# Column sums of the odd units on GpSimd, and seven split units instead of three, in the first product of a graph network

## The reference

```
h = relu(layernorm(x)); x = x + relu([h, adj @ h] @ W.T + b)           # layer 0
h = relu(layernorm(x)); a = adj + I; d = rsqrt(sum(a, axis=-1))        # layer 1
x = x + unit_rows((a * d[:, None] * d[None, :]) @ h @ W.T + b)
h = relu(layernorm(x)); x = x + GRU(relu(adj @ h @ Wm.T + bm), h)      # layer 2
h = relu(layernorm(x)); z, its 4 nearest rows of all 4096,             # layer 3
x = x + d2 * ((S + adj) @ (d2 * h)) @ W2 + b2
```

## Time and profile before

| | before |
|---|---|
| median of three runs | 1536.28 us |
| profiled execution, from its first to its last instruction (its span; no other time of it is given) | 1534.6 us |
| first product, block period of blocks 1 to 7 | 29.95 us |
| busy over the span: TensorE, VectorE, ScalarE, GpSimd | 96%, 78%, 52%, 12% |
| in a block of the first product: TensorE, VectorE, ScalarE | 29.95, 26.84, 6.17 us |

### The profile page before, as it was taken

How to read it: one execution, slowest core, us unless ns; L and a number is a source line. 1 busy time by engine, 2 the same in 40 slices (tenths; PEclk the granted TensorE clock), 3 DMA queues, 4 the chain that set the end, 5 groups by cost and what they waited for, 6 DMA issues and landing times.

```text
span 1534.6 us, 18912 instructions
## 1 busy us (share of the span) xinstructions
PE 1466.8 (96%) x4982; PEld 841.8 (55%) x4982; DVE 1193.8 (78%) x1644; ACT 797.9 (52%) x1243; POOL 191.1 (12%) x205
## 2 busy tenths in 40 slices
PE   7999999999999999999999999999999999698894
PEld 4555555677776667666766662222222224466662
DVE  7899989878787776677778776888888887576784
ACT  3212223566666666566565644445455545566673
POOL 0000000000000000000000000000000000888886
PEclk9999999999999999999999999999999999899997
DMA  8788888898898677777898990000000006889992
GB/s 306 253 284 273 286 277 290 311 328 329 330 339 333 239 282 281 271 255 272 302 336 324 336 334 24 0 7 7 7 7 7 7 0 223 286 312 331 337 344 95
DMA packets 99515, 351.64 MB, mean 229 GB/s; under 512 B 12704, under 2 KB 12832, under 8 KB 99488
## 3 DMA queue, kind: packets, MB, share of 16 engines
q1 hardware_dynamic: 94752, 340.83, 62.3%
q0 software_dynamic: 4736, 10.49, 2.0%
HBM read 347.08 MB, written 4.19 MB: 229 GB/s over the span
## 4 chain that ended last, share of the span: by engine, by line
PE 81%; POOL 11%; issue 5%; DMA 1%; DVE 1%; ACT 0%; POOLq 0%; SPq 0%; ACTq 0%
PE ps L529 17%; PE ps L354 12%; PE ps L386 11%; POOL landing L1151 10%; PE ps L390 9%; PE ps L392 9%; PE ps L391 8%; PE ps L530 5%; PE ps L448 1%; PE ps L414 1%; PE ps L474 1%; PE ps L475 1%; POOL picks L1148 1%; PE ps L421 1%; PE ps L347 1%
## 5 line engine op out<-in xcount | busy, mean ns | idle before, releaser
L981 DVE TENSOR_TENSOR A_lo<-ring,A_hi 128x1024 fp32r<-128x1024 f32 x411 | 488.6, 1220 | 137.7 <-ACT A_hi L573 125.5
L573 ACT ACTIVATE A_hi<-ring 128x1024 fp32r<-128x1024 f32 x411 | 425.0, 1055 | 151.3 <-PE ps L392 83.9
L390 PE MATMUL ps<-A_hi,G_odd_hi 128*128 128x512 f32 x588 | 268.3, 456 | 36.6 <-DVE A_lo L981 35.7
L392 PE MATMUL ps<-A_hi,G_odd_lo 128*128 128x512 f32 x588 | 235.5, 401 | 0.0
L391 PE MATMUL ps<-A_lo,G_odd_hi 128*128 128x512 f32 x588 | 235.1, 400 | 0.0
L354 PE MATMUL ps<-ring,G_first 128*128 128x512 f32 x428 | 190.7, 592 | 0.0
L1055 DVE MAX8 rows_T<-scores 128x8 f32<-128x4096 f32 x32 | 141.7, 4428 | 57.9 <-ACT scores L573 57.9
L386 PE MATMUL ps<-ring,G_whole 128*128 128x512 f32 x384 | 180.4, 592 | 0.0
L1140 POOL DMA_DIRECT2D scaled_rows<-G_last x8 | 6.2, 780 | 1291.1 <-ACT G_last L573 1291.1
L1151 POOL DMA_INDIRECT landing<-scaled_rows,picks x128 | 159.4, 1246 | 35.0 <-issue 30.7
L390 PEld LDWEIGHTS ps<-A_hi,G_odd_hi 128*128 128x128 f32 x588 | 114.1, 194 | 87.8 <-issue 38.5
(11 more groups left out here) (143 smaller groups left out, 1547.5 us busy)
## 6 DMA issues: line engine op xcount, KB each, us to landing
ring<-adj_t SPq DMA_DIRECT2D x640, 512.0 KB
X<-x_rows SPq DMA_DIRECT2D x8, 256.0 KB, 7.9
scaled_rows<-G_last POOLq DMA_DIRECT2D x8, 256.0 KB, 2.7
landing<-scaled_rows,picks POOLq DMA_INDIRECT x128
out_rows<-X SPq DMA_DIRECT2D x8, 256.0 KB
pack<-packed SPq DMA_DIRECT2D x1, 836.0 KB, 13.7
pack<-packed SPq DMA_DIRECT2D x1, 192.0 KB, 3.3
```

Source lines behind the costliest of these rows:

```text
L390: mm(acc, G_hi[odd][:, m, kk, :], hi, start=begin, stop=False)
L392: last = mm(acc, G_lo[odd][:, m, kk, :], hi, start=False, stop=end)
L573: return nc.scalar.activation(out_ap, in_ap, func, **k)
L981: v.tensor_tensor(A_lo[:, slot, :, :], ring[:, u % SLOTS, :, :], A_hi[:, slot, :, :].bitcast(fp32), ALU.subtract).then_inc(lower_ready, 1)
```

## The change

The odd units leave VectorE's loop. GpSimd gets a loop of its own, `sum_odd_pieces`, whose first instruction adds units 1 and 3 into the second half of `colsum`, and six further ones add units 5 to 15 (one instruction of 128 x 1024 for each). The one semaphore `summed` becomes `even_summed` (raised by VectorE in steps of 2) and `odd_summed` (raised by GpSimd, by 4 for the first, by 2 for each later one). The loads of odd slots wait for `odd_summed`. The first product splits seven units of blocks 1 to 7 instead of three, all of them odd. Two tables of steps change with it.

```diff
-SPLIT_FIRST = (7, 10, 14)
+SPLIT_FIRST = (1, 3, 5, 7, 9, 11, 13)
...
-                    sp.wait_ge(summed, last + 1)
+                    sp.wait_ge(odd_summed if u % 2 else even_summed, last + 1)
...
                 for u in range(UNITS):
-                    dve.wait_ge(at_loaded[u % SLOTS], loaded_value(b, u))
-                    half = colsum[:, u % 2 * UK:u % 2 * UK + UK, :]
-                    if u < 2:
-                        ins = v.tensor_copy(half, ring[:, u % SLOTS, :, :])
-                    else:
-                        dve.wait_ge(summed, UNITS * b + u - 1)
-                        ins = v.tensor_tensor(half, half, ring[:, u % SLOTS, :, :], ALU.add)
-                    ins.then_inc(summed, 1)
+                    half = colsum[:, 0:UK, :]
+                    if u % 2 == 0:
+                        dve.wait_ge(at_loaded[u % SLOTS], loaded_value(b, u))
+                        if u == 0:
+                            ins = v.tensor_copy(half, ring[:, u % SLOTS, :, :])
+                        else:
+                            dve.wait_ge(even_summed, UNITS * b + u)
+                            ins = v.tensor_tensor(half, half, ring[:, u % SLOTS, :, :], ALU.add)
+                        ins.then_inc(even_summed, 2)
                     if u in split_units(0, b):
                         lower(0, b, u)
...
-                dve.wait_ge(summed, UNITS * (b + 1))
+                dve.wait_ge(even_summed, UNITS * (b + 1))
+                dve.wait_ge(odd_summed, UNITS * (b + 1))
...
+            def sum_odd_pieces(b):
+                half = colsum[:, UK:2 * UK, :]
+                pool.wait_ge(at_loaded[1], loaded_value(b, 1))
+                pool.wait_ge(at_loaded[3], loaded_value(b, 3))
+                if not (isinstance(b, int) and b == 0):
+                    pool.wait_ge(colsum_ready, b)
+                g.tensor_tensor(half, ring[:, 1, :, :], ring[:, 3, :, :], ALU.add).then_inc(odd_summed, 4)
+                for u in range(5, UNITS, 2):
+                    pool.wait_ge(at_loaded[u % SLOTS], loaded_value(b, u))
+                    pool.wait_ge(odd_summed, UNITS * b + u - 1)
+                    g.tensor_tensor(half, half, ring[:, u % SLOTS, :, :], ALU.add).then_inc(odd_summed, 2)
+            sum_odd_pieces(0)
+            with pool.Fori(1, NB) as b:
+                sum_odd_pieces(b)
...
-PE_FIRST, ACT_FIRST, DVE_FIRST = (0, 7, 10), (0, 1, 7, 10, 13), (5, 7, 9, 15)
+PE_FIRST, ACT_FIRST, DVE_FIRST = (0, 9, 11), (0, 5, 7, 10, 13), (5, 7, 9, 15)
```

More of the change, by code:

```diff
@@ L205, in gnn_stack @@
         at_loaded = [sem(f"at_loaded{s}") for s in range(SLOTS)]
-        used, summed = sem("used"), sem("summed")
+        used, even_summed, odd_summed = sem("used"), sem("even_summed"), sem("odd_summed")
         upper_ready, lower_ready = sem("upper_ready"), sem("lower_ready")
@@ L285, in load_block @@
                         sp.wait_ge(used, held)
-                        sp.wait_ge(summed, held)
+                        sp.wait_ge(odd_summed if lu % 2 else even_summed, held)
                     elif lu in whole_units(lp, lb):
```

## The result

The changed kernel takes 1605.05 us (median; 1602.2 to 1605.45) against 1536.29 us: a ratio of 1.044, 95% interval 1.0416 to 1.0465. The forecast was slower, 1582 in a range of 1538 to 1620: right in sign and cause, 23 us short in size.

The account below looks back on a forecast made before the run. TensorE was taken to bound the first product, VectorE close behind. To the profiled 1534.6 us, GpSimd's port holds added 43 over seven blocks and block 0 added 3: 1581, as median 1582, range 1538 to 1620.

Parts of the forecast that it names:

- TensorE's saving: Blocks 1 to 7: four more split units save TensorE 1.3 us a block, 9.0 us in seven blocks.
- the wait at unit 11: Blocks 1 to 7: TensorE waits 1.3 us a block for unit 11's A_lo, delayed behind rectify; 9 us in all.
- A: First product: long GpSimd adds let VectorE through, so saving and unit 11 wait cancel; 1536 us, chance 0.13.
- B: First product: no port effect and no TensorE wait at unit 11, so the full 9 us come; 1527 us, chance 0.05.
- The port: SBUF: GpSimd reads and VectorE instructions with two SBUF inputs block each other for the whole instruction.
- The length of GpSimd's add: First product: a 128 x 1024 add on GpSimd takes 2.4 us, twice VectorE's 1.22.
- Rival C: First product: GpSimd's add costs 3.7 us, at least 43.8 us a block; 1640 us in all, chance 0.08.
- low end D: First product: port held, but GpSimd's add takes 1.22 us; block 31.1, total 1545; included in the forecast's 0.74.
- The block: Blocks 1 to 7: period 36.1 us, middle of 34.7 (port alone) and 37.4 (VectorE's path); 43 us over seven blocks.
- TensorE's waits: Blocks 1 to 7: TensorE waits some 7 us a block for A_lo.
- The clock: TensorE's granted clock: stays at full, so no time was added for it.
- Block 0: First block: one VectorE add goes and one GpSimd add comes per pair, over six pairs; 3 us of 0 to 8.

Follow-up runs that it names:

- the adds for nobody: Kernel before, plus seven GpSimd adds of free 128 x 1024 tiles a block, unawaited until the first product ends: 1635.3 us, ratio 1.0617.
- the writes: Changed kernel with GpSimd's adds cut to one element and two 128 x 1024 memsets added for each odd unit: 1543.1 us, ratio 1.0035.
- the tiny adds: Changed kernel with GpSimd's adds cut to one element per partition, all waits and orders kept: 1538.8 us, ratio 1.0008.

## Why the prediction was right, and where it was short

**TensorE's saving and the wait at unit 11** were right to a few tenths of a microsecond: without the port load the block is 30.1 (29.9 forecast), the wait 1.2 (1.3), and without the wait 28.6 (28.6). So rivals A and B were right as to what the schedule would do; they were wrong only in that the port is free.

**The port** was read rightly from GpSimd's tiny instructions: a long add holds VectorE's two-input instructions until it ends, shown in the timeline, by the adds for nobody, and by the writes, which hold hn alone.

**The length of GpSimd's add** was 2.35 us against the 2.4 taken. Rival C (3.7) and the low end D (1.22) are out.

**The block** failed in size: 39.2 instead of 36.1, and that is the term seven x 6.1 = 43, which measured 64.8. It was the middle between a lower end (34.7, the port alone) and an upper one (37.4, VectorE's path). The lower end took the port for a pool that fills up, and counted only instructions with two SBUF inputs (17.9 us); the copy and the four tensor_scalar of hn wait for the port too and were stretched by 2.2 and 3.8 us in the block shown. What counts is the path with the holds put in. The path alone would have given 1591 (7.45 x 7 = 52 in place of 43), and it was itself too short, by two errors that partly cancel. I take them apart in the block shown, 38.5 us.

The holds on the path were less than forecast. A_lo, adds, hn and copy together were stretched by some 11.9 us, of 7 x 2.35 = 16.4 that GpSimd's adds hold. The copy's 2.2 of it fell in the gap at the turn, as I had let the first add do: VectorE still waited 0.86 us for A_hi of unit 1 behind it. That leaves 9.7 on the path, where I had 11.1.

The rest of the path was longer: 38.5 - 9.7 = 28.8 us, where I had 26.3. Most of that is one stretch. I followed VectorE on to A_lo of unit 13 and took TensorE from there, but TensorE didn't wait for it (VectorE's A_lo of 11 and 13, then TensorE's start of unit 13):

```profile
161.40 1.22 DVE L983 TENSOR_TENSOR A_lo<-ring,A_hi 128x1024 fp32r<-128x1024 f32 x1 [1.30 <-ACT A_hi L573]
163.67 1.22 DVE L983 TENSOR_TENSOR A_lo<-ring,A_hi 128x1024 fp32r<-128x1024 f32 x1
...
166.53 0.79 PE L345 MATMUL ps<-A_hi,G_first_hi 128*128 128x512 f32 x1
```

A_lo of unit 13 was there at 164.89 us, and TensorE came to it at 166.53; in all seven blocks it came 1.5 to 2.5 us after. From A_lo of unit 11 on, the path is TensorE's: unit 11, the operand step and unit 12 are 1.40 + 0.9 + 1.72 = 4.0 us, where I had an add and a subtraction, 2.3. My own sentence that unit 13 comes late by nothing said so. That is 1.7 of the 2.5 us; the clock had some 0.3 here, and for the last 0.5 I have no account.

**TensorE's waits** of some 7 us a block were right in sum (38.50 - 31.66 = 6.8 in the block shown), but half of them, 3.4 us, were for hn and not for A_lo. Over the first product, 60 to 330 us, hn had a third:

```profile
PE ps L345 <- DVE A_lo L983: 32.5, 29, 3.2
PE ps L421 <- DVE hn L821: 16.2, 7, 3.5
```

**The clock** I left at full. In the changed kernel it went to the lower level once in each of the seven blocks, each time in or close behind a wait of TensorE of 2.9 to 3.5 us. With the tiny adds it stayed at full, and there TensorE takes 3.49 us from its transposes to unit 11 and 3.70 from unit 11 to unit 13. The changed kernel takes 3.55 to 4.01 and 3.70 to 4.67. The differences over seven blocks add up to 2.3 and 2.0 us: an estimate of 4.3 us of the 64.8 for the clock.

**Block 0** was 2.2 us longer (3 forecast, 0 to 8), and what follows the first product grew by 1 us (0 forecast).

## What to carry to other kernels

Don't count GpSimd as free time beside a busy VectorE. An elementwise add of SBUF data that GpSimd takes over costs VectorE up to GpSimd's whole duration (2.35 us) to save it 1.14, and in the block shown 72% of it landed. Give GpSimd work that only writes (hn alone suffered from that here), or put it where VectorE waits, or works with one input in PSUM as for X, and look for the holds in the durations of VectorE's own instructions, since a held instruction counts as busy and not as idle.

Before splitting more work among engines in a fixed order, walk one block with each engine's list: an instruction that stands behind a step which waits for another engine (A_hi of unit 11 behind rectify) can give back exactly what the change saves. And at each point ask which engine arrives last: a path that stays on one engine to its end (VectorE to A_lo of unit 13) can miss that another has taken over (TensorE from unit 11).

## What was not expected of the hardware

The four instructions of hn, 1.1 us together, grew to 4.9 beside two GpSimd adds in a row, and doubled (342 to 690 ns) in the mean beside memsets of 951 ns. A copy of 692 ns grew to 2848 ns when it started 0.05 us behind a GpSimd add of 2.35. So VectorE's quick one-input instructions suffer more for their length than the two-input ones, and hn is the only one seen held by writes too (no memset began ahead of a copy).
